# A block-local attention and MoE block in 20 overlapped slots: dividing the attention output with channels on partitions, and splitting the scores of four more steps

## The reference

```python
x = x + attn(layernorm(x))      # 16 heads of 8 channels, block-local
x = x + ffn(layernorm(x))       # 16 experts, 4 chosen, and a shared one

def attn(x):                    # in blocks of 64 tokens, each sees itself and the block before
    q, k, v = (x @ Wq.T, x @ Wk.T, x @ Wv.T)            # by head
    scores = where(mask, q @ k.T / sqrt(8), -1e30)      # mask: j > i and j <= i + 64
    p = softmax(scores)
    return (p @ v).merge_heads() @ Wo.T

def ffn(x):
    w = top-4 weights of sigmoid(x @ gate) + bias, 2 of 4 groups, normalised, times 2.5
    y = sum_e w[e] * ((silu(x @ w_gate[e]) * (x @ w_up[e])) @ w_down[e])
    return y + (silu(x @ sw_gate) * (x @ sw_up)) @ sw_down
```

## Time and profile before

| | us |
|---|---|
| median of 3 runs | 706.51 (700.37 to 708.97) |
| the profiled execution | 704.78 |
| its span, from the first to the last instruction | 703.0 |

### The profile page before, as it was taken

One profiled execution on the slowest core, in us unless ns is written; L12 is line 12 of the kernel. 1 busy time (PEld: TensorE's weight loads), 2 busy tenths in 40 slices (PEclk: granted clock), 3 DMA queues, 4 the chain that ended last, 5 costly groups with the idle time before them and its releaser, 6 DMA issues.

```text
span 703.0 us, 20018 instructions
## 1 busy us (share of the span) xinstructions
PE 664.9 (95%) x6488; PEld 522.0 (74%) x6488; DVE 588.0 (84%) x1708; ACT 529.9 (75%) x1635; POOL 477.3 (68%) x599
## 2 busy tenths in 40 slices
PE   3988779999999999999999999999999999989996
PEld 2776558777777777777777777777777777767875
DVE  2688796998989798998989798998989798887763
ACT  3787767787887879787887878787887878764332
POOL 3504156877878687877878687877878687776533
PEclk9999979999999999999999999999999999999999
DMA  6010023041313214050313214050313213041321
GB/s 176 1 33 31 1 70 99 5 151 33 122 60 106 75 51 130 3 149 30 121 60 106 75 50 130 2 149 30 121 60 106 75 47 110 13 135 35 120 77 46
DMA packets 50246, 52.60 MB, mean 75 GB/s; under 512 B 5665, under 2 KB 31905, under 8 KB 50081
## 3 DMA queue, kind: packets, MB, share of 16 engines
q1 hardware_dynamic: 50208, 52.14, 24.3%
HBM read 43.20 MB, written 4.72 MB: 68 GB/s over the span
## 4 chain that ended last, share of the span: by engine, by line
PE 65%; ACT 16%; DVE 9%; issue 5%; DMA 2%; POOL 2%; DVEq 0%; POOLq 0%; ACTq 0%; SPq 0%
PE PS L1057 12%; PE PS L865 9%; PE PS L903 8%; PE PS L867 8%; PE PS L866 7%; ACT probs L603 7%; PE PS L994 5%; ACT q_by_head L554 3%; PE PS L891 3%; PE PS L1027 3%; PE PS L1054 2%; PE PS L933 2%; DVE neg_max L778 2%; DVE sums L748 2%; DVE probsT L738 1%
## 5 line engine op out<-in xcount | busy, mean ns | idle before, releaser
L603 ACT ACTIVATE probs<-PS,neg_max 128x96 f32<-128x96 f32 (+1 forms) x1024 | 247.0, 351 | 82.4 <-DVE neg_max L778 82.4
L477 POOL TENSOR_TENSOR gate<-gate,spread 128x512 f32<-128x512 f32 x124 | 158.3, 1276 | 110.4 <-ACT gate L554 49.8
L482 POOL TENSOR_TENSOR hh<-gate,tu 128x512 f32<-128x512 f32 x108 | 139.3, 1290 | 14.1 <-DVE tu L767 6.6
L1057 PE MATMUL PS<-wd,hh 128*128 128x128 f32 x1024 | 138.5, 278 | 6.9 <-POOL hh L482 4.9
L1057 PEld LDWEIGHTS PS<-wd,hh 128*128 128x128 f32 x1024 | 126.8, 192 | 15.8 <-issue 6.4
L767 DVE SCALAR_TENSOR_TENSOR tu<-th,PS 128x512 f32<-128x512 f32 x128 | 87.2, 681 | 55.3 <-ACT th L570 46.7
L778 DVE TENSOR_REDUCE neg_max<-PS 128x4 f32<-128x384 f32 (+1 forms) x256 | 121.5, 513 | 12.1 <-PE PS L903 10.8
L865 PE MATMUL PS<-x_hi,w_hi 128*128 128x512 f32 x288 | 125.2, 435 | 0.0
L570 ACT ACTIVATE th<-PS 128x512 f32<-128x512 f32 x128 | 80.4, 628 | 48.1 <-PE PS L867 46.6
L738 DVE STREAM_TRANSPOSE probsT<-probs 128x768 f32<-128x768 f32 (+1 forms) x128 | 114.5, 894 | 0.0
L867 PE MATMUL PS<-x_lo,w_hi 128*128 128x512 f32 x288 | 114.4, 397 | 0.0
(11 more groups left out here) (108 smaller groups left out, 992.2 us busy)
## 6 DMA issues: line engine op xcount, KB each, us to landing
spread<-weights_by_expert SPq DMA_DIRECT2D x248, 128.0 KB, 3.0
X<-x SPq DMA_DIRECT2D x32, 256.0 KB, 3.6
OUT<-H SPq DMA_DIRECT2D x16, 256.0 KB, 3.1
out<-OUT SPq DMA_DIRECT2D x16, 256.0 KB, 3.9
ffn_stage<-w_gu SPq DMA_DIRECT2D x1, 1152.0 KB, 7.0
wd<-w_down SPq DMA_DIRECT2D x1, 512.0 KB, 7.2
weights_by_expert<-cT SPq DMA_DIRECT2D x16, 32.0 KB, 1.6
probsT<-w_att SPq DMA_DIRECT2D x1, 192.0 KB, 3.1
```

Source lines behind the costliest of these rows:

```text
L477: tt(gate2[:, :], gate[:, k % 2, :], spread[:, k % SP_BUFS, :], ALU.mult).then_inc(s_g2, 1)
L482: tt(hh[:, k % 2, :], gate2[:, :], tu[:, k % 2, :], ALU.mult).then_inc(s_h, 1)
L603: ins = nc.scalar.activation(probs[:, u % PROB_BUFS, tt, 2 * rows + e, j0:KW], PS[:, rows, n * KW + j0:n * KW + KW], ACT.Exp, bias=neg_max ...
L1057: ins = mm(PS[:, 7, r], hh[:, k % 2, r], wd[:, k, :], start=(k == 0 and n == 0), stop=(k == NP - 1), skip_group_check=True)
```

## The change

**The division.** The output stays with channels on partitions. VectorE takes the reciprocal of `sums` in place and turns it (`turn_sums`, at `TURN`, step 6 of the half b = 0 and step 0 for b = 1). GpSimd multiplies the turned reciprocals, which lie with (head, block) on partitions, with a mask `block_of` into `by_block`, 128 x 8 x 32, one column for each token (`EXPAND`, steps 7 and 1). OT, now in step 7 (and 3), is a single fp32 product of `by_block` with a constant map `to_channel` that adds up the one right row for each channel. VectorE multiplies `o_f` by that PSUM bank into `oT`. The transposes, the four small products, ON and ScalarE's copy go. The map is built in slot 0 on VectorE and GpSimd.

**The filling.** Half by half scores and the products that nothing reads also run in steps 0 to 3 of slot 3 (`warming`), and there are 8 of the latter instead of 6.

```diff
-OT, ON, OW = 14, 15, 16
+TURN = (14, 16)
+EXPAND = (15, 17)
+OT, OW = 15, 16
...
-    (POST, (OT, OT + 4, ON, ON + 4, OW, OW + 4, SH)), (WEIGHTS, (CT,)))
+    (POST, (OT, OT + 4, OW, OW + 4, SH)), (WEIGHTS, (CT,)))
...
+def warming(slot, s):
+
+    return filling(slot) or slot.fixed and slot.n == 3 and s < FF % STEPS
...
-BUSY = 6
+BUSY = 8
...
+                    for b, stage in enumerate(EXPAND):
+                        g, _ = at(sl, s, stage)
+                        if g:
+                            if not (g.fixed and g.n == 0):
+                                taken(pool, slot_before(sl), (OT + 4 * b) % STEPS, POST)
+                            pool.wait_ge(s_sum_t, g.n * GB + b + 1)
+                            whole = [P, NQ, Q]
+                            tt(by_block[:, b, :, :], sums_t[:, b, :].unsqueeze(1).broadcast_to(whole),
+                               block_of[:, :].unsqueeze(2).broadcast_to(whole), ALU.mult).then_inc(s_exp, 1)
...
+                        for a in range(4):
+                            shape = [P, 4, D]
+                            ins = tt(to_channel[:, 32 * a:32 * a + 32].rearrange("p (v d) -> p v d", d=D),
+                                     lane_of[:, a:a + 1].unsqueeze(2).broadcast_to(shape),
+                                     grouprow.unsqueeze(2).broadcast_to(shape), ALU.mult)
...
-                    g, b = at(sl, s, ON, 4, GB)
-                    if g:
-                        side, bank = filled(act, sl, s, POST)
-                        copy(oT[:, :], bank[:, 0:T]).then_inc(s_taken[side], 1)
...
+                    def turn_sums(b):
+                        g, _ = at(sl, s, TURN[b])
+                        if g:
+                            dve.wait_ge(s_sum, g.n * NU + 4 * b + 4)
+                            link(sl, v_.reciprocal(sums[:, b, :], sums[:, b, :]))
+                            v_.transpose(sums_t[:, b, :], sums[:, b, :]).then_inc(s_sum_t, 1)
...
-                        link(sl, v_.reciprocal(o_rs[:, :, :], bank[:, T:T + Q].rearrange("p (a v) -> p a v", v=4)))
-                        v_.tensor_tensor(o_n[:, :, :].rearrange("p n (a v d) -> p (n a) v d", v=4, d=D),
...
+                        dve.wait_ge(s_o, g.n * GB + b + 1)
+                        v_.tensor_tensor(oT[:, :], o_f[:, :], bank[:, 0:T], ALU.mult).then_inc(s_taken[side], 1)
...
+                    turn_sums(0)
                     sum_probs()
+                    turn_sums(1)
...
+                        pe.wait_ge(s_exp, g.n * GB + b + 1)
+                        mm(bank[:, 0:T], to_channel[:, :], by_block[:, b, :, :].rearrange("p t q -> p (t q)"),
+                           start=True, stop=True).then_inc(s_filled[side], 1)
```

More of the change, by code:

```diff
@@ L220, in preln_block_kernel @@
         o_f = sb("o_f", [P, T])
-        o_rs = sb("o_rs", [P, 8, 4])
-        o_n = sb("o_n", [P, 2, P])
+        lane_of = sb("lane_of", [P, 4])
+        block_of = sb("block_of", [P, NQ])
+        to_channel = sb("to_channel", [P, P])
+        by_block = sb("by_block", [P, GB, NQ, Q])
         oT = sb("oT", [P, T])
@@ L275, in preln_block_kernel @@
         grouprow = const("grouprow")
-        sums_of = ident.rearrange("p (v h c a) -> p c h a v", v=4, h=2, c=4)
         def by_lane(n):
@@ L327, in preln_block_kernel @@
         s_sum_t = sem("sums_turned")
+        s_lane = sem("lane_masks_ready")
+        s_chan = sem("channel_map_ready")
+        s_exp = sem("reciprocals_by_block")
         s_o_ps = sem("o_in_psum")
@@ L727, in slot @@
                         v_.tensor_copy(ident4[:, :], const("ident4"))
+                        v_.tensor_reduce(block_of[:, :], ident.rearrange("p (v t a) -> p t v a", t=NQ, a=HG),
+                                         mybir.AxisListType.XY, ALU.add)
+                        v_.tensor_reduce(lane_of[:, :], ident.rearrange("p (x a) -> p a x", a=HG),
+                                         AX_X, ALU.add).then_inc(s_lane, 1)
                         dve.wait_ge(s_cst, 1)
@@ L799, in slot @@
                         side, bank = filled(dve, sl, s, POST)
-                        link(sl, v_.reciprocal(o_rs[:, :, :], bank[:, T:T + Q].rearrange("p (a v) -> p a v", v=4)))
-                        v_.tensor_tensor(o_n[:, :, :].rearrange("p n (a v d) -> p (n a) v d", v=4, d=D),
-                                         bank[:, 0:T].rearrange("p (a v d) -> p a v d", v=4, d=D),
-                                         o_rs[:, :, :].unsqueeze(3).broadcast_to([P, 8, 4, D]),
-                                         ALU.mult).then_inc(s_taken[side], 1)
+                        dve.wait_ge(s_o, g.n * GB + b + 1)
+                        v_.tensor_tensor(oT[:, :], o_f[:, :], bank[:, 0:T], ALU.mult).then_inc(s_taken[side], 1)
                     g, b = at(sl, s, OW, 4, GB)
@@ L934, in slot @@
                         ins.then_inc(s_filled[side], 1)
-                    if filling(sl) and at(sl, s, SC, 1, NU)[0]:
+                    if warming(sl, s) and at(sl, s, SC, 1, NU)[0]:
                         for _ in range(BUSY):
@@ L957, in slot @@
                             taken(pe, slot_before(sl), KP % STEPS, LATE)
-                        if filling(sl):
+                        if warming(sl, s):
                             for rows in range(2):
@@ L987, in slot @@
                         if not later and not (g.fixed and g.n == 0 and b == 0):
-                            pe.wait_ge(s_o, g.n * GB + b)
+                            taken(pe, slot_before(sl) if b else sl, (OT if b else OT + 4) % STEPS, POST)
                         pe.wait_ge(s_pt, g.n * NU + 4 * b + (4 if later else 3))
@@ L1003, in slot @@
                         side, bank = free(POST)
-                        pe.wait_ge(s_o, g.n * GB + b + 1)
-                        for half in range(2):
-                            nc.tensor.transpose(bank[:, P * half:P * half + P], o_f[:, P * half:P * half + P], ident)
-                        pe.wait_ge(s_sum_t, g.n * GB + b + 1)
-                        for c in range(4):
-                            ins = mm(PS[32 * c:32 * c + 32, RING[side], T:T + Q], sums_t[:, b, :], sums_of[:, c, :, :, :],
-                                     start=True, stop=True)
-                        ins.then_inc(s_filled[side], 1)
-                    g, b = at(sl, s, ON, 4, GB)
-                    if g:
-                        side, bank = free(POST)
-                        taken(pe, sl, (s - 1) % STEPS, POST)
-                        for half in range(2):
-                            ins = nc.tensor.transpose(bank[:, P * half:P * half + P], o_n[:, half, :], ident)
-                        ins.then_inc(s_filled[side], 1)
+                        if g.fixed and g.n == 0:
+                            pe.wait_ge(s_chan, 1)
+                        pe.wait_ge(s_exp, g.n * GB + b + 1)
+                        mm(bank[:, 0:T], to_channel[:, :], by_block[:, b, :, :].rearrange("p t q -> p (t q)"),
+                           start=True, stop=True).then_inc(s_filled[side], 1)
                     g, b = at(sl, s, OW, 4, GB)
@@ L1021, in slot @@
                         side, bank = free(POST)
-                        taken(pe, slot_before(sl) if s == 0 else sl, (s - 1) % STEPS, POST)
+                        taken(pe, sl if b else slot_before(sl), (OT + 4 * b) % STEPS, POST)
                         if g.fixed and g.n == 0 and b == 0:
```

5 lines of the change are left out of this document (2 added, 3 removed).

## The result

The changed kernel takes 714.77 us, the median of four runs (714.4 to 716.35), against 705.13 (700.37 to 708.97) for the kernel before in the same comparison: ratio 1.0155, 95% interval 1.0122 to 1.0188. The forecast was 713. The profiled execution of the changed kernel took 714.96 us with a span of 713.2, so 10.2 us more span than before.

A forecast was written before the change was run, and what follows sets the result against it. TensorE, busy 95% of the span, was taken as the bound. From 704.78 us: +1.00 for the first logits wait, +11.4 for 12 slots at 0.95, about nothing for draining, -4.0 for the filling gave 713 us; range 697 to 722.

The forecast's parts named there:

- The mechanism: Loop steps 0 and 3: logits matmul and routing-weight transposes wait for VectorE's `oT` to free their bank; slot +0.95 us.
- The new matmul: Steps 7 and 3 on TensorE: one fp32 matmul of 128 x 256 comes in, taken as 0.52 us.
- The reciprocal: VectorE's reciprocal in SBUF, taken as 0.25 us, between 0.168 and 0.349; the skill's formula estimated 0.19.
- The passes removed, -0.70 a slot: TensorE, steps 6, 7, 2 and 3: transposes and sums matmuls go, the new matmul comes; net -0.35 us per half.
- such a wait for step 7: Scores of step 7: TensorE meets the exponentials only 0.21 us earlier, then waits for VectorE's product anyway.
- The waits: Ring of two PSUM banks: TensorE waits 1.00 us at the logits and 0.42 at the routing weights per slot.
- LG's 1.00: Logits matmul, step 0: starts at 275.84 instead of 274.84, waiting for VectorE's product behind `tu` and both maxima; +1.00 us.
- CT's 0.42 less 0.1: Routing-weight transposes, step 3: start at 255.97 instead of 255.54, waiting for `oT`; some 0.1 us of it covered.
- The clock in the loop: Rival: waits idle TensorE and its clock falls in each slot, 1.7 us each, giving 735 us; chance 0.03.
- The filling: Filling slots ahead of the loop: steadier clock and shorter division chain less added dummies, -4.0 us; bounds 0 and 6.
- the gain in slot 3: Slot 3 of the filling: clock staying at 2.4 GHz gives back 1.0, 1.0 and 1.2 us in three windows.
- My charge of 0.9 for two dummies more: Filling: two more dummies on the path in four steps, at most 1.4 us, of which 0.9 was taken.

The follow-up runs named there:

- experiment 4: Changed kernel with TensorE's reciprocal product written to the free half of PV's bank, outside the ring of two, with semaphores of its own: 691.51 us.
- experiments 2 and 3: Changed kernel with VectorE's product `oT` moved earlier for one half only: step 7 alone 707.61 us, step 3 alone 710.09 us.
- experiment 1: Changed kernel with VectorE's product `oT` moved ahead of the maxima (step 7) and ahead of `tu` (step 3): 698.22 us.
- experiment 5: Kernel before with only its copy of `oT` moved from ScalarE, ahead of the exponentials, to VectorE, behind the maxima: 733.24 us.
- the filling's part alone: Kernel before with only the filling's edits (eight dummies, `warming` in slot 3): 729.4 us, its loop code being reloaded.
- the division alone, moved: Changed kernel with the filling as before and 128 instructions of nothing on TensorE ahead of everything: 729.4 us.
- the kernel with five dummies: Kernel before with dummies and scores half by half also in steps 0 to 3 of slot 3, five dummies instead of six: 705.1 us.

## Why the prediction was right, point by point

**The mechanism holds.** LG and CT wait for `oT`, by row and by experiment: with the product first the kernel is 16.6 us faster, with a bank of its own 23.3, and the same wait put into the kernel before costs it 29 us together with what it does to the clock.

**The new matmul.** 0.54 from start to start (271.78 to 272.32); forecast 0.52. The reciprocal takes 0.31; forecast 0.25. Of the two rows that bounded it, the one from PSUM, 0.349, was the nearer. The Trainium skill (page "VectorE: DVE Perf Modes", section "The TRN2 errata — SBUF-src ops pay a fixed extra latency per instruction") gives (N+151)/0.96 ns for an fp32 `tensor_tensor` add; the prediction put it on a reciprocal. The trace does not agree there: 0.31 was measured and 0.19 is that estimate, while `tu` with 512 elements took the 0.69 that the formula gives.

**The passes removed, -0.70 a slot: the term that was mis-sized in the loop.** The work fell as forecast: in the slot shown TensorE is busy 38.66 us against 39.35, and from start to start it is 2 x (0.59 + 0.28 - 0.54) = 0.66. But time came back for only 0.50 of it, as experiment 4 shows, where nothing waits for `oT` (39.09 on average against 39.59). Freed of the transposes, TensorE reaches the scores early and waits 0.42 and 0.27 for exponentials. The prediction saw such a wait for step 7 (0.21 us earlier and no more), and took it as hidden behind LG's. It should have been taken off the saving itself.

**The waits were right in sum.** From the slot without the ring's turn (39.09) to the changed one (40.72) it is 1.63. Forecast were LG's 1.00 and the 0.35 saved ahead of it, and CT's 0.42 less 0.1: 1.67 (with it a slot is +0.97, which the forecast rounded to 0.95). Within the sum CT was too cheap (0.52 by experiments 2 and 3, for 0.32) and LG too dear (0.77, and 0.34 that experiment 1 leaves in place and experiment 4 takes away, for 1.35). So the slot became +1.13 for the forecast +0.95, and nearly all of the difference is the saving.

**The clock in the loop** had a chance of 0.03, as a fall in each slot, and came as a fall in one slot of twelve, worth 1.5 us. So the loop cost 15.3 (12 x 1.13, this, and a first slot 0.3 longer than its like) instead of 11.4. The Trainium skill (page "TensorE: Matmul & The Clock Gate", section "A second HAM failure mode: psum-queue depth-cycling") warns of a clock that goes down and up again in a kernel that turns through PSUM banks. The traces agree in part: in the changed kernel once, and with longer waits (experiment 5) three times.

**The filling: -4.0 forecast, -6.1 measured** (-5.1 with LG's wait inside, which costs some 1.0), at the bound of 6. The step that was mis-sized is the gain in slot 3, which I had put down to the clock. I priced three windows of it with 3.2 us and took the slow stretch at 105 to 109 as one that stays. It went too: over the whole of slot 3 the granted clock was 0.83 before, and 1.00 with the filling's part alone. Three windows of the kernel before that lie beside those of the earlier trace rows:

```profile
80.00:85.00 5.00, 4.63 (x64) 3.31 (x56) 3.41 (x7) 3.00 (x12) 0.04 (x1) 0.87 0.02 5
85.00:90.00 5.00, 1.58 (x20) 1.05 (x20) 4.76 (x28) 3.51 (x15) 2.56 (x6) 0.81 0.00 0
105.00:110.00 5.00, 5.00 (x23) 4.07 (x24) 2.09 (x5) 3.12 (x6) 4.38 (x6) 0.66 0.52 147
```

From 75 to 95 and 105 to 110 us it lost 0.21, 0.13, 0.19, 0.50 and 0.34 of 5 us each, 6.9 in all. That is a bound, since TensorE was partly idle there (busy 1.58 of 5 from 85 to 90). With the filling's part alone slot 3 became 5.2 shorter (35.7 for 40.9). My charge of 0.9 for two dummies more was too high: eight against six cost 0.25 (111.27 against 111.02). How much of the 5.2 is the clock and how much the scores going half by half is not shown. CT of slot 3 came 2.6 us earlier (90.89 for 93.47), not 4: its own wait and the other half of the clock's gain lie behind it.

**The sum.** 1.0 + 11.4 - 4.0 = +8.4 was forecast and +10.2 came: the loop was 3.9 dearer, the filling 2.1 cheaper. The two errors cancel in part, so the time is closer than the steps are. That draining costs nothing holds to 0.1 us.

**Luck in the forecast.** It never asked where TensorE's loop would lie in its program. Had it come to lie 128 instructions further on, the same change would have measured some 741, outside the range of 697 to 722.

## What to carry to other kernels

When a buffer is handed round in strict turn, the price of a use is set by where its last reader stands in that reader's queue. Removing work from the bound engine can gain nothing if the turn now ends behind a long operation elsewhere: move the reader forward, or take the short use out of the ring (here 16.6 and 23.3 us for one moved instruction, or half a bank that lay unused). Before a kernel with a hardware loop is compared with a variant of itself, look at the instruction packets in both profiles: if they differ, the code's place is being measured along with the change.

## What the runs showed of the hardware

- TensorE's code for a loop of 1,618 to 1,702 instructions is kept over the jump back in some places of the program and loaded again in others. It was kept where the loop began 5 to 28 instructions past a multiple of 256 and ended 108 to 179 past one; it was loaded again where it began 53 to 156 past and ended 219, 238 or 43 past. Start and end moved together, so these runs do not tell which counts. The cost was 2.4 to 4.4 us of idle time at a jump, and as much again in places from the clock that fell behind it.
- The Trainium skill (page "Runtime: NRT & Kernel Launch", section "Instruction fetch mechanics") gives 2048 instructions for that memory, in blocks of 256, the next block being fetched while one runs. That would fit these cases if code fetched ahead from behind the loop takes room from the loop's own; no run here shows that directly. Its window of two blocks does not fit them.
- A wait on a semaphore that is already satisfied is not free on TensorE. In the division alone, moved, the loads had landed when ScalarE's first operation on them started, at 5.97 us (the row below), and TensorE's first transposes started at 19.90: 13.9 us for 128 instructions of two waits, 109 ns each as an estimate. Eight more such instructions took 0.6 us more (20.52), 80 ns each. Of the 13.9 us only 11.1 delayed the kernel, since without the padding TensorE waited for its input until 8.77.

```profile
5.97 0.62 ACT L581 ACTIVATE w_hi<-probsT 128x256 fp32r<-128x256 f32 x2 [3.96 <-DMA probsT<-consts]
```

- In the first 36 us the profile's granted clock reads 1.00 while five dummies take 1.43 us; at 40.48 us they take 0.75. There the durations tell the speed, not the clock. A window of the kernel with five dummies in which they took 1.43:

```profile
25.00:30.00 5.00, 5.00 (x24) 4.24 (x24) 1.99 (x4) 2.54 (x11) 2.10 (x1) 1.00 0.00 0
```

- A stretch at the lower clock came behind an idle time of 1 us in one slot of twelve (42.2 us, also in the division alone, moved), with the same wait in all of them. What picks the slot stays open.
